# Four V products every fourth step instead of two every second, in an attention and feed-forward block on one Trainium2 core

## The reference

```
x = x + attention(layernorm(x)) @ Wout + bout     # 16 heads of 64, rotary embedding on the first 32 of each
x = x + ((gelu(layernorm(x) @ U1 @ V1 + b1)) @ U2 @ V2 + b2)      # rank 32, inner width 512
attention: sim = rope(q) @ rope(k).T / 8; softmax over the keys; @ v
```

## Time and profile before

| | us |
|---|---|
| median of 3 runs (1443.5 to 1446.81) | 1446.76 |
| the profiled execution | 1446.73 |
| its span, first to last instruction | 1444.9 |
| TensorE matmul, busy | 1380.5 (96%) |
| VectorE, busy | 1171.5 (81%) |
| GpSimd, busy | 977.9 (68%) |
| ScalarE, busy | 788.8 (55%) |

### The profile page before, as it was taken

One profiled execution on the slowest core, in us unless ns is written; L12 is line 12 of the kernel. 1 busy time (PEld: TensorE's weight loads), 2 busy tenths in 40 slices (PEclk: granted clock), 3 DMA queues, 4 the chain that ended last, 5 costly groups with the idle time before them and its releaser, 6 DMA issues.

```text
span 1444.9 us, 25614 instructions
## 1 busy us (share of the span) xinstructions
PE 1380.5 (96%) x7313; PEld 501.1 (35%) x7313; DVE 1171.5 (81%) x1320; ACT 788.8 (55%) x1511; POOL 977.9 (68%) x487
## 2 busy tenths in 40 slices
PE   3688999999999999999999999999999999999897
PEld 1123333332433333342333333243333334233334
DVE  6876888878888888888888887888888788888844
ACT  3245555646555555555555565555555555555456
POOL 4397677848677685858667684867768585874641
PEclk9699999999999999999999999999999999999999
DMA  5403122130312222031312213031222203131002
GB/s 160 88 1 81 23 60 59 36 82 15 80 35 60 44 59 59 15 80 37 80 22 59 58 33 84 15 80 33 60 46 59 59 15 80 37 80 23 15 16 59
DMA packets 78770, 75.47 MB, mean 52 GB/s; under 512 B 36020, under 2 KB 45752, under 8 KB 78488
## 3 DMA queue, kind: packets, MB, share of 16 engines
q1 hardware_dynamic: 77296, 74.15, 23.2%
q10 hardware_dynamic: 1448, 1.00, 0.3%
HBM read 22.04 MB, written 2.35 MB: 17 GB/s over the span
## 4 chain that ended last, share of the span: by engine, by line
PE 50%; issue 22%; POOL 19%; DVE 6%; ACT 2%; DMA 1%; POOLq 0%; SPq 0%; ACTq 0%; DVEq 0%
PE O L390 17%; PE S L378 9%; PE S L379 8%; POOL SA L682 7%; PE M L401 5%; POOL T L658 5%; PE TILE L308 3%; PE TILE L332 3%; POOL STAGE L669 3%; POOL YR L661 3%; DVE MX L608 2%; ACT PF L515 1%; PE TILE L324 1%; PE TILE L314 1%; POOL QK L804 1%
## 5 line engine op out<-in xcount | busy, mean ns | idle before, releaser
L682 POOL TENSOR_TENSOR SA<-PF 128x1024 f32<-128x1024 f32 x254 | 656.6, 2592 | 370.0 <-DVE SUM L615 310.1
L515 ACT ACTIVATE PF<-S 128x512 f32<-128x512 f32 x1024 | 556.1, 597 | 449.6 <-PE S L379 448.0
L608 DVE TENSOR_REDUCE MX<-M 128x1 f32<-128x1024 f32 x508 | 597.6, 1218 | 167.5 <-PE M L401 165.6
L390 PE MATMUL O<-PF,V 128*64 128x512 f32 x2048 | 499.7, 609 | 0.0
L378 PE MATMUL S<-QK 128*128 128x512 f16 x1024 | 393.8, 385 | 7.9 <-ACT PF L515 7.9
L379 PE MATMUL S<-QK 128*128 128x512 f16 x1024 | 389.7, 381 | 0.0
L618 DVE TENSOR_TENSOR SUM<-SUM,SA 128x1024 f32<-128x1024 f32 x126 | 227.7, 1807 | 6.0 <-POOL SA L682 4.9
L390 PEld LDWEIGHTS O<-PF,V 128*64 128x64 f32 x2048 | 125.0, 137 | 251.1 <-issue 176.2
L378 PEld LDWEIGHTS S<-QK 128*128 128x128 f16 x1024 | 99.4, 97 | 264.0 <-ACT PF L515 112.3
L401 PE MATMUL M<-QK 64*128 64x512 f16 x1016 | 161.5, 395 | 15.5 <-DMA QK<-STAGE 9.8
L497 ACT ACTIVATE OS<-O 64x512 f32<-64x512 f32 x128 | 75.8, 592 | 83.3 <-PE O L390 82.6
(11 more groups left out here) (108 smaller groups left out, 743.9 us busy)
## 6 DMA issues: line engine op xcount, KB each, us to landing
QK<-STAGE SPq DMA_DIRECT2D x128, 256.0 KB, 3.9
QK<-STAGE SPq DMA_DIRECT2D x128, 128.0 KB, 3.1
RB<-den SPq DMA_DIRECT2D x124, 128.0 KB, 3.0
X<-in_L_attn_queries SPq DMA_DIRECT2D x4, 512.0 KB, 13.1
QK<-MN SPq DMA_DIRECT2D x128, 1.0 KB, 2.0
out<-X SPq DMA_DIRECT2D x8, 256.0 KB, 2.3
RT<-DS SPq DMA_DIRECT2D x124, 2.0 KB, 1.7
WRAW<-in_L_attn_Wkv SPq DMA_DIRECT2D x1, 1024.0 KB, 9.4
```

Source lines behind the costliest of these rows:

```text
L390: mm = e.matmul(O[DH * z:DH * z + DH, :], V[:, h, kt * DH:(kt + 1) * DH], PF[:, t % SLOTS, z * HALF:(z + 1) * HALF], start=(kt == 0), stop ...
L515: e.activation(PF[:, t % SLOTS, z * HALF:(z + 1) * HALF], S[:, z * HALF:(z + 1) * HALF], ACT.Exp, scale=EXP_SCALE).then_inc(exped, 1)
L608: e.tensor_reduce(MX[:, place % 2, q:q + 1], bank, AX, ALU.max).then_inc(max_read, 1)
L682: e.tensor_tensor(SA[:, (t // 2) % 2, :], PF[:, t % SLOTS, :], PF[:, t % SLOTS + 1, :], ALU.add).then_inc(two_summed, 1)
```

## The change

The four products of the steps t - 4 to t - 1 stand in every fourth step, ahead of its units; units stay in every even step. BETWEEN = -0.5 gives tiles half steps. A tile at 4n - 0.5 stands between the second and the third of the four products of step 4n: the rot tiles, and some of the turn_x and down tiles. The pass tiles and out tiles stand at the even steps in the middle of the group, the V and den tiles, which only ScalarE reads, at steps that are multiples of four. Out tile (0, 0) moves from step 28 to 26, a den tile from 6 to 4, V tiles from 16, 17, 24, 26 to 8, 12, 24, 28. ScalarE's act_rot follows the exponentials of the steps 3, 7, 11 and 15; GpSimd's rot_low and rot_add of a step stand before its sum.

```
-QK_AT = (0, 2, 4, 7, 8, 10, 12, 14)
-V_AT = {16: (1, 0), 17: (1, 1), 24: (0, 0), 26: (0, 1)}
-DEN_AT = {6: 1, 20: 0}
+BETWEEN = -0.5
+QK_AT = (0 + BETWEEN, 2, 4 + BETWEEN, 6, 8 + BETWEEN, 10, 12 + BETWEEN, 14)
+V_AT = {8: (1, 0), 12: (1, 1), 24: (0, 0), 28: (0, 1)}
+DEN_AT = {4: 1, 20: 0}
-OUT_AT = {18: (1, 0), 22: (1, 1), 28: (0, 0), 30: (0, 1)}
+OUT_AT = {18: (1, 0), 22: (1, 1), 26: (0, 0), 30: (0, 1)}
-TURN_X0_AT = (6, 18, 21, 22, 25, 27)
-TURN_X_AT = (4, 7, 8, 10, 12, 14)
-DOWN_AT = (19, 21, 23, 24, 26, 29)
+TURN_X0_AT = (16 + BETWEEN, 18, 20 + BETWEEN, 22, 24 + BETWEEN, 28 + BETWEEN)
+TURN_X_AT = (4 + BETWEEN, 6, 8 + BETWEEN, 10, 12 + BETWEEN, 14)
+DOWN_AT = (16 + BETWEEN, 20 + BETWEEN, 24 + BETWEEN, 24, 28 + BETWEEN, 28)
...
         def pe_step(e, it, t):
             u = t + LEAD
-            if t % 2 == 0:
-                for back in (t - PV_LAG, t - PV_LAG + 1):
+            if t % 4 == 0:
+                for back in range(t - PV_LAG, t):
+                    if back == t - PV_LAG + 2:
+                        pe_tiles(e, it, t + BETWEEN)
                     if back >= 0:
                         pe_values(e, it.step(back), it.i * GH + back // KT, back, it.i)
                     elif not it.first:
                         pe_values(e, it.step(back), it.i * GH - 1, back + STEPS, it.i - 1)
+            if t % 2 == 0:
                 if not (it.last and u >= STEPS):
                     pe_next_unit(e, it, u)
                     pe_next_unit(e, it, u + 1)
...
         def act_step(e, it, t):
             n, h, kt = it.step(t), t // KT, t % KT
+            act_tiles(e, it, t + BETWEEN)
             if kt == 2 and (not it.first or h > 0):
                 act_copy_out(e, it.i * GH + h - 1, (h - 1) % GH)
...
             act_tiles(e, it, t)
+            for n, kind, args in it.at(t - 3 + BETWEEN):
+                if kind == "proj" and args[2] == "rot":
+                    act_rot(e, args, it.i + 1)
...
         def dve_step(e, it, t):
...
+            dve_tiles(e, it, t + BETWEEN)
...
         def pool_step(e, it, t):
...
-            for n, kind, args in it.at(t - 4):
+            for n, kind, args in it.at(t - 4 + BETWEEN):
                 if kind == "proj" and args[2] == "rot":
                     rot_low(e, args, it.i + 1)
-            for n, kind, args in it.at(t - 1):
+            for n, kind, args in it.at(t + BETWEEN):
                 if kind == "proj" and args[2] == "rot":
                     rot_add(e, args, it.i + 1)
```

More of the change, by code:

```diff
@@ L64, in tiles_of @@
     out = []
-    for t in range(STEPS):
+    for t in (n / 2 if n % 2 else n // 2 for n in range(-1, 2 * STEPS)):
         if t in QK_AT and not last:
@@ L486, in act_tiles @@
                     act_den(e, it.pair(args), made, bank)
-            for n, kind, args in it.at(t - 3):
-                if kind == "proj" and args[2] == "rot":
-                    act_rot(e, args, it.i + 1)
         def act_copy_out(e, head, h):
```

## The result

The change makes the kernel slower: 1494.97 us (median of 4, 1494.64 to 1496.9) against 1446.01 for the kernel before on the same chip, a ratio of 1.0342 with a 95% interval of 1.0327 to 1.0357. The forecast was 1471 us, +24 (the loop +24.5, the first iteration -1.5, the last +1); measured are +49 between the medians and +47.9 between the spans of the two profiled executions.

A forecast was written before the change was run, and what follows sets the result against it. TensorE was taken to bound the kernel in the fourteen loop iterations; 1446.7 us, +24.5 for the loop (+1.75 per iteration), -1.5 for the first iteration and +1 for the last made 1471 us, own range 1458 to 1484.

The forecast's parts named there:

- rival 1: Step 25's sum meets a GpSimd addition, so normalising is late: stall 2.05 instead of 0.7, 1490 us, chance 0.18.
- four runs of four products: Four V-product groups without a tile in the middle save 0.16 us each: -0.64 per loop iteration.
- tile between products, four times: Rotation tiles before steps 0, 4, 8, 12 cut the runs, costing 0.10 us each: +0.4 per iteration.
- old stalls gone: Stalls at steps 16 and 17 and ScalarE's wait for the rotated sum all go: -1.0 us per iteration.
- empty steps 0 and 16: Without a tile, the next scores wait for exponentials, 0.49 us at each step: +0.98 per iteration.
- copy of O before steps 3, 11, 19: ScalarE's copy delays exponentials and so TensorE's scores: +1.3 us per iteration, with ends of 0.55 and 2.05.
- output tile at 26: The tile waits for VectorE's normalising product of step 25: +0.7 us per iteration, with ends of 0.3 and 2.05.
- rival 2: Hardly a change: units after scores cost 0.21 and normalising is in time; +0.55 us per iteration, 1449 us, chance 0.10.
- the first part: First iteration, bound by GpSimd up to the keys' hand-over: first tile some 3 us earlier; -1.5 us, ends -6 and +3.
- the last iteration: Three stalls of 0.49 from step 20, fewer shape changes, layer-norm tiles waiting as before: +1 us, ends -4 and +6.
- The cost put at nothing: Earlier denominator, moved V tiles, keys' hand-over and TensorE's waits for VectorE's maxima in the loop: no cost taken.
- Rivals 2 and 3: The second as above; the third: copy of O delays no scores, neither copy nor output tile stalls, 1428 us, chance 0.10.

The follow-up runs named there:

- e2_out_28: The kernel after with output tile (0,0) back at step 28 and its V tile at 26: 1482.16 us.
- e3_turn_late: The kernel after with the last iteration's turn_x tiles at steps 6, 7, 10, 11, 14, 15, out of the products: 1494.68 us.
- e8_written_out: The kernel after with all sixteen iterations written out instead of a loop, the work the same: 1497.75 us.
- e1_copy_first: The kernel after with ScalarE's copy of O two steps earlier, ahead of the exponentials of steps 0, 8, 16, 24: 1482.71 us.
- e5_four_copy: The kernel before with four products every fourth step and ScalarE's copy of O two steps earlier: 1446.26 us.
- e4_four_alone: The kernel before with four products every fourth step and nothing else changed: 1462.72 us.
- e6_copy_out28: The kernel after with the copy of O two steps earlier, output tile (0,0) at step 28 and V tile (0,1) at 26: 1464.05 us.

## Why the prediction was right in direction and half in size

The measured 1494.97 lies outside the forecast's own range (1458 to 1484) and in that of rival 1 (1484 to 1505), but not by rival 1's lock in the loop. The loop's terms, per iteration, as forecast and as the trace after has them (start to start, against the unhindered distances of the earlier trace rows):

| term | forecast | measured |
|---|---|---|
| four runs of four products | -0.64 | -0.61 (3.59 each) |
| tile between products, four times | +0.4 | +0.4 (0.75 instead of 0.64) |
| old stalls gone | -1.0 | -0.99 (what is left of the sum) |
| empty steps 0 and 16 | +0.98 | +1.25 (0.67 and 0.58) |
| copy of O before steps 3, 11, 19 | +1.3 | +1.63 (0.72, 0.56, 0.35) |
| output tile at 26 | +0.7 | +1.05 |
| wait in the products of step 4 | 0 | +0.11 |
| sum | +1.75 | +2.84 |

The sum is that of the stretches, 1196.58 / 14 - 82.63 = 2.84. The old stalls were not measured by themselves: the other terms make +3.83, and what is left is -0.99.

*Right:* the four products, the cut runs, and scores before units at 0.96, that is 0.09 more than four matmuls at 0.21 to 0.22, in all places; the tail's 0.21, which rival 2 rested on, does not hold in the loop. By the rule of the Trainium skill ("TensorE: Matmul & The Clock Gate", "Part 3: Packing small matmuls — row/col tiling") that a weight load overlaps a running matmul only in other rows of the array, units after scores always pay; the trace agrees here, and not in the tail, and the page has no size for it. Right too that each of the three stalls exists, at its place and with its releaser, that the copy's stall at step 27 was under the output tile's wait (e2_out_28), and the sign of the first part. That it is -1.4 against -1.5 is luck in part: the first tile comes 2.7 earlier as forecast (56.10 against 58.77), but e3_turn_late, with the same first iteration, ends it 0.8 before the kernel after does.

*Mis-sized, in part for one cause:* "Empty steps" was priced from the earlier trace rows, which is the last iteration, written out. There the exponentials start 0.64 after the scores; in the loop 0.83 at step 0 and 0.73 at step 16. The prediction's own rows had a 0.73 of the loop (714.15 to 714.88), and it used both. e8_written_out brings steps 0 and 16 back to 1.29, so the loop's form costs 0.18 and 0.09; that it is the waits, which compare with a register in the loop and with a constant outside, was only argued. The copy of O begins 671.03 - 667.67 = 3.36 after step 0's scores where the working had 2.99: 0.22 of this are the later scores and exponentials of step 1, and 0.15 are that the copy starts 1.11 after these (669.92 to 671.03), not 0.96. Scores go on in the bank of step 2 at 5.23 (672.90) instead of 4.85, and TensorE is there at 4.58 instead of 4.39, so a stall of 0.46 becomes 0.65, and 0.05 at the second half 0.07. The three stalls make 1.63 instead of 1.3. Written out, the first of them is 0.52 and the other two are as in the loop, so the form has 0.13 of the 0.33.

*Output tile at 26:* the sum was short, as chosen (1.31), and the norm ends 4.62 after step 24's scores where the working had 4.59. The terms left out are 0.26 between the norm's end (736.04) and the first matmul (736.30), whose weights are the norm's output, and 0.10 in the tile.

*Failed: the last iteration,* +1 forecast with -4 to +6 around it, +9.6 measured. The prediction said that its layer-norm tiles "wait for VectorE as before" and gave the output tile no wait there. TensorE's idle time in that iteration is 14.2 us against 5.2 before, which is 9.0 of the 9.6. For the layer norm's tiles it waits 8.0 instead of 3.1: the tiles between products come earlier than before, and it waits 1.7, 1.9 and 3.2 us at steps 3.5, 7.5 and 11.5 and 0.3 and 0.9 at steps 6 and 10. For the output tile it waits 3.7 instead of nothing, for exponentials 2.4 instead of 1.0, and a wait of 1.0 for the denominator tile is gone. Its busy time differs by 0.55 only, with a clock of 0.95 after and 0.96 before.

The wait of 3.7 holds rival 1's mechanism, wrong in the loop, right in this one iteration where bias additions fill GpSimd: the norm of 2.28 ended at 1431.79, 1.08 after the addition's 1430.71. Sum and norm together lost 2.1 against 1.21 each; what made the rest of the 3.7 was not found. The Trainium skill ("SBUF — State Buffer", "Who interferes with whom") lets a VectorE instruction with two SBUF inputs wait for a GpSimd one that reads; the trace agrees in four places, each ending 1.08 after GpSimd: the earlier trace rows, e1_copy_first's sum (752.17 and 751.09), and sum and norm of the last iteration. So do all 79 sums and norms of the kernel after, of 223, that last more than 1.4 us (1.08 or 1.09).

*The cost put at nothing* was nothing only while the copy's stalls stood before it. VectorE had slack because TensorE came late: with the stalls removed, e1_copy_first waits 0.72 in step 4, e5_four_copy up to 0.91 at the units. Rivals 2 and 3, "hardly a change" and "faster" both needed the copy or the output tile in time; neither was.

So it is not TensorE's own work in groups that made it slow, but the waits that came with them. The grouping puts a head's copy of O in TensorE's way (2.1 per iteration in e4_four_alone, more than the 1.2 that eight runs of four save), because products that finish a head now end ahead of exponentials that ScalarE has to do first; the moved tiles add two empty steps and a late output tile. With the copy first, the output tile at 28, GpSimd's addition behind its sums and a tile on every step that needs one, runs of four are 1.0% faster than the kernel before. What stays open is why TensorE's clock falls behind a wait in one execution and not in another.

## What to carry to other kernels

When work of the bounding engine is grouped, write down for each other engine what it now receives together and what its fixed order puts in front: here one copy, 1.2 us long, in front of exponentials cost more than four groups saved. Leave no step of the bounding engine bare when the next one waits on a round trip through another engine; give such steps the independent tiles before placing tiles anywhere else. Read a latency in the same form of code as it will run in (a loop's from the loop), and look at the first and last iterations by themselves: here one of sixteen gave a fifth of the loss.

## What the runs showed of the hardware that was not expected

- Exponentials start 0.83 us after the scores of step 0 in the loop and 0.64 where the same kernel has its loop written out; up to the next scores it is 1.47 against 1.29. At step 16 it is 0.73 against 0.64. In steps 20 to 25 the two differ less, 0.63 to 0.73 against 0.63 to 0.69.
- A VectorE sum or norm that meets a GpSimd addition ends 1.08 us after it (2.25 to 3.06 long instead of 1.21); putting GpSimd's other addition behind the sum took it back to 1.22.
- TensorE's granted clock fell behind some waits of about 2 to 4 us and not behind others. It fell to 0.50 behind 3.71 in the kernel after, two products took 3.57 instead of 1.94 behind 3.15, and in the kernel before it was 0.50 over the 2.20 us behind 3.09, this row. But behind the same wait of 3.15 it stayed at 1.00 in e2_out_28, and in e6_copy_out28 too, where it fell behind waits of 2.33 (0.72 over the next 3.6 us) and 1.87 (0.63 over the next 3.9) instead. TensorE's busy time in the last iteration is 77.3 where the clock never fell (e2_out_28) and 80.6 where it was 0.96 (e6_copy_out28).

```profile
1341.82 1.09 PE L340 MATMUL TILE<-IDENT,WRAW 128*128 128x128 f32 x4 [3.09 <-DVE WRAW L281]
```
